# Attention on one Trainium2 core: row maxima over pairs of PSUM banks, and the matmuls of a pair issued one behind the other

## The reference, cut to what matters

```
def _attention(q, k, v, bias):
    scores = einsum('bhqd,bhkd->bhqk', q, k) / sqrt(hd)
    if bias is not None:
        scores = scores + bias[None, None]
    return einsum('bhqk,bhkd->bhqd', softmax(scores), v)

pos = arange(L)
decay_bias = -abs(pos[None, :] - pos[:, None]) * (1.0 - decay_factor)
out_short = _attention(q, k_s, v_s, decay_bias)
out_long = _attention(q, k_l, v_l, None)
out = alpha * out_short + (1.0 - alpha) * out_long      # alpha = sigmoid(mix_weight)
```

## Time and profile before

| | |
|---|---|
| median of 3 runs | 4903.04 us |
| span of the profiled execution | 4900.3 us |
| PE busy | 4717.9 us, 96% |
| DVE busy | 4038.9 us, 82% |
| ACT busy | 2978.9 us, 61% |
| attention stage, first to last V | 546.4 to 3786.9 us of the span |

### The profile page before, as it was taken

One profiled execution on the slowest core, in us unless ns is written; L12 is line 12 of the kernel. 1 busy time (PEld: TensorE's weight loads), 2 busy tenths in 40 slices (PEclk: granted clock), 3 DMA queues, 4 the chain that ended last, 5 costly groups with the idle time before them and its releaser, 6 DMA issues. The chain is left out here.

```text
span 4900.3 us, 100056 instructions
## 1 busy us (share of the span) xinstructions
PE 4717.9 (96%) x30796; PEld 2078.4 (42%) x30796; DVE 4038.9 (82%) x6609; ACT 2978.9 (61%) x5170; POOL 3278.9 (67%) x1267
## 2 busy tenths in 40 slices
PE   8998999999999999999999999999998699999998
PEld 3444333333333333333333333333332477777776
DVE  7567888888888888888888888888884488888887
ACT  3222477777777767777777777767766355555554
POOL 0000498998989989898998989989898233333332
PEclk9999799999999999999999999999999799999999
DMA  5444366666666666666666676666755100000000
GB/s 171 126 140 130 92 149 153 152 154 158 147 156 151 152 157 147 160 146 158 152 153 157 145 160 152 152 153 145 165 134 114 67 27 21 27 27 27 27 23 12
DMA packets 207465, 592.51 MB, mean 121 GB/s; under 512 B 37043, under 2 KB 110899, under 8 KB 157941
## 3 DMA queue, kind: packets, MB, share of 16 engines
q0 software_dynamic: 55008, 400.58, 37.4%
q1 hardware_dynamic: 151919, 185.58, 12.6%
q10 hardware_dynamic: 38, 0.08, 0.0%
HBM read 123.56 MB, written 61.64 MB: 38 GB/s over the span
## 5 line engine op out<-in xcount | busy, mean ns | idle before, releaser
L877 DVE TENSOR_REDUCE rowmax_parts<-scores_qk 128x1 f32<-128x512 f32 x4096 | 2525.9, 681 | 427.0 <-PE scores_qk L954 426.8
L862 ACT ACTIVATE probs_T<-scores_kq 128x512 f32<-128x512 f32 x4096 | 2288.4, 597 | 955.4 <-PE scores_kq L954 857.7
L800 POOL TENSOR_TENSOR probs_added<-probs_added,probs_T 128x2048 f32<-128x2048 f32 x510 | 2387.0, 4680 | 49.5 <-POOL probs_added L800 35.7
L954 PE MATMUL scores_kq<-q_operand,k_operand 103*128 103x512 f16 (+3 forms) x3712 | 1274.6, 349 | 19.5 <-ACT probs_T L862 17.4
L954 PE MATMUL scores_qk<-k_operand,q_operand 96*128 96x512 f16 (+4 forms) x3712 | 1121.6, 351 | 42.4 <-DMA v_operand<-v_dram 15.0
L1025 PE MATMUL outputs_T<-probs_T,v_operand 128*32 128x512 f32 x8192 | 1092.7, 605 | 1.3 <-ACT probs_T L862 1.3
L954 PEld LDWEIGHTS scores_kq<-q_operand,k_operand 103*128 103x128 f16 x3712 | 358.4, 97 | 934.6 <-ACT probs_T L862 688.0
L954 PEld LDWEIGHTS scores_qk<-k_operand,q_operand 96*128 96x128 f16 (+1 forms) x3712 | 354.6, 98 | 432.0 <-DVE rowmax_parts L877 186.6
L1650 PE MATMUL f_gate_up<-w_gate_up,xq_T 128*128 128x256 f16 (+1 forms) x4608 | 494.3, 266 | 7.7 <-DVE hidden L1541 6.6
L812 POOL DMA_DIRECT2D probs_poured<-probs_T x318 | 276.7, 870 | 266.1 <-DMA probs_poured<-probs_T 192.8
L1650 PEld LDWEIGHTS f_gate_up<-w_gate_up,xq_T 128*128 128x128 f16 x4608 | 421.4, 99 | 76.8 <-issue 24.3
(11 more groups left out here) (167 smaller groups left out, 4134.8 us busy)
## 6 DMA issues: line engine op xcount, KB each, us to landing
probs_poured<-probs_T POOLq DMA_DIRECT2D x382, 1024.0 KB, 7.6
qk_parts_dram<-qk_parts SPq DMA_DIRECT2D x96, 256.0 KB, 2.8
q_operand<-qk_parts_dram SPq DMA_DIRECT2D x192, 128.0 KB, 2.6
k_operand<-qk_parts_dram SPq DMA_DIRECT2D x192, 128.0 KB, 4.0
v_dram<-v_heads SPq DMA_DIRECT2D x16, 1024.0 KB, 6.5
v_operand<-v_dram SPq DMA_DIRECT2D x64, 256.0 KB, 6.1
q_operand_above<-qk_parts_dram SPq DMA_DIRECT2D x96, 128.0 KB, 2.9
x_groups<-x SPq DMA_DIRECT2D x8, 1024.0 KB, 9.3
```

The lines of the kernel that those rows point to most:

```text
L800: nc.gpsimd.tensor_tensor(total, first, probs[:, b % PBUF, :], ALU.add).then_inc(added.sem, 1)
L862: nc.scalar.activation(probs[:, kb % PBUF, qt * BANK:(qt + 1) * BANK], pb[:, k % 2, :], ACT.Exp)\
L877: nc.vector.reduce_max(rowmax[:, w % 2, c // NQ, c % NQ:c % NQ + 1], pa[:, k % 3, :], AX.X)\
L954: return nc.tensor.matmul(out, lhsT, rhs, start=start, stop=stop, skip_group_check=True)
```

## The change

The tile `turned` is gone, and its bank makes `scores_qk` four banks: two pairs. Two neighbouring M chunks are written into the two banks of a pair; only the first of them waits and only the second signals. VectorE reduces a pair with one instruction of 1024 elements. TensorE's order becomes V, E2, M0, M1, E3, E0, M2, M3, E1. The turning of the maxima moves from TensorE and ScalarE to VectorE, as a transpose of 32 x 32 blocks in SBUF on fp16 values, behind the first pair of step 10; each block of 32 queries is then placed by a DMA of its own, so four DMAs instead of one for each destination. VectorE's transpose waits for the negation and for the DMAs that last read the buffer it writes. GpSimd clears `negmax` once at the start. The diff, cut to its core:

```diff
-        negmax = sb("negmax", [P, 2, KB], F32)
-        maxT = sb("negmax_T", [KB, 2, P], F16)
+        negmax = sb("negmax", [P, 2, SQUARE], F16)
+        maxT = sb("negmax_T", [P, 2, SQUARE], F16)
-        pa = ps("scores_qk", [P, 3, BANK], F32)
+        pa = ps("scores_qk", [P, 4, BANK], F32)
-        pt = ps("turned", [P, BANK], F32)
...
             def place_max(w, n):
-                sp.wait_ge(roundm.sem, roundm.at(n, w + 1))
+                sp.wait_ge(turned.sem, turned.at(n, w + 1))
                 for dst in (q_op[w], q_up[w]) if w % 2 == 0 else (q_op[w],):
-                    sp.dma_start(dst[MROW:MROW + 1, :], maxT[:, w % 2, :]).then_inc(maxrow[w].sem, 16)
+                    row = dst[MROW:MROW + 1, :].rearrange("o (t b c) -> o t b c", t=KB, c=SQUARE)
+                    for b in range(P // SQUARE):
+                        sp.dma_start(row[:, :, b, :], maxT[b * SQUARE:b * SQUARE + KB, w % 2, :]).then_inc(maxrow[w].sem, 16)
...
-            def max_chunk(w, n, c):
-                nc.vector.reduce_max(rowmax[:, w % 2, c // NQ, c % NQ:c % NQ + 1], pa[:, k % 3, :], AX.X)\
+            def max_pair(w, n, g):
+                k = w * PAIRS + g
+                dve.wait_ge(scoredA.sem, scoredA.at(n, k + 1))
+                half = pa[:, 2 * (k % 2):2 * (k % 2) + 2, :].rearrange("p b q -> p (b q)")
+                nc.vector.reduce_max(rowmax[:, w % 2, g // 2, g % 2:g % 2 + 1], half, AX.X).then_inc(maxed.sem, 1)
...
+            def turn_max(w, n):
+                dve.wait_ge(maxed.sem, maxed.at(n, (w + 1) * (PAIRS + 1)))
...
+                nc.vector.transpose(maxT[:, w % 2, :], negmax[:, w % 2, :]).then_inc(turned.sem, 1)
...
             def scores_for_max(w, n, c):
-                if k >= 3:
-                    pe.wait_ge(maxed.sem, maxed.at(n, k - 2 + (k - 3) // CHUNKS))
+                if c % 2 == 0 and k >= 2:
+                    pe.wait_ge(maxed.sem, maxed.at(n, k - 1 + (k - 2) // PAIRS))
...
-                last.then_inc(scoredA.sem, 1)
+                if c % 2:
+                    last.then_inc(scoredA.sem, 1)
...
                         scores(i + 1, 2)
                         maxima(0)
+                        maxima(1)
                         scores(i + 1, 3)
-                        maxima(1)
-                        if ahead and i == TURN_MAX:
-                            turn_max(*ahead)
+                        scores(i + 2, 0)
                         maxima(2)
-                        scores(i + 2, 0)
                         maxima(3)
                         scores(i + 2, 1)
```

More of the change, by code:

```diff
@@ L583 @@
 CHUNKS = KB * NQ
+PAIRS = CHUNKS // 2
 UNITS = 4
@@ L594 @@
 TURN_MAX = 10
+SQUARE = 32
 INVERT = 7
@@ L641, in attend @@
         poured_sum = sb("probs_poured", [P, 2, L], F32)
-        rowmax = sb("rowmax_parts", [P, 2, KB, NQ], F32)
-        negmax = sb("negmax", [P, 2, KB], F32)
-        maxT = sb("negmax_T", [KB, 2, P], F16)
+        rowmax = sb("rowmax_parts", [P, 2, KB, 2], F32)
+        negmax = sb("negmax", [P, 2, SQUARE], F16)
+        maxT = sb("negmax_T", [P, 2, SQUARE], F16)
         oT = sb("o_T", [P, 2, BANK], F32)
@@ L655, in attend @@
         pc = ps("sums", [P, BANK], F32)
-        pt = ps("turned", [P, BANK], F32)
         consts = sem("a_consts")
         chain = sem("a_const_chain")
+        cleared = sem("a_negmax_cleared")
         rows = [sem(f"a_rows{i}") for i in range(2)]
@@ L664, in attend @@
         opened = [Rises(sem(f"a_opened{w}"), 10 - 3 * (w % 2), 16) for w in range(UNITS)]
-        maxrow = [Rises(sem(f"a_maxrow{w}"), 2 - w % 2, 16) for w in range(UNITS)]
-        scoredA = Rises(sem("a_scored_qk"), UNITS * CHUNKS)
-        maxed = Rises(sem("a_maxed"), UNITS * (CHUNKS + 1), credit=1)
+        maxrow = [Rises(sem(f"a_maxrow{w}"), 4 * (2 - w % 2), 16) for w in range(UNITS)]
+        scoredA = Rises(sem("a_scored_qk"), UNITS * PAIRS)
+        maxed = Rises(sem("a_maxed"), UNITS * (PAIRS + 1), credit=1)
         turned = Rises(sem("a_max_turned"), UNITS)
-        roundm = Rises(sem("a_max_rounded"), UNITS)
         scoredB = Rises(sem("a_scored_kq"), UNITS * CHUNKS)
@@ L777, in _ @@
             nc.gpsimd.memset(ones[:, :], 1.0).then_inc(consts, 1)
+            nc.gpsimd.memset(negmax[:, :, :], 0.0).then_inc(cleared, 1)
             nc.gpsimd.memset(ident[:, :], 0.0).then_inc(chain, 1)
@@ L831, in _ @@
         def _(act):
[L832 to L840, removed]
             load_positions(act, 0)
-            round_max(0, 0)
             def one_pass(n, first, last):
@@ L847, in one_pass @@
                     for kb in range(KB):
-                        if kb == (TURN_MAX + 2) % KB and after(w, n, last):
-                            round_max(*after(w, n, last))
                         u, b = divmod(w * KB + kb - PBUF, KB)
@@ L872, in _, with negate @@
         def _(dve):
-            def max_chunk(w, n, c):
-                k = w * CHUNKS + c
+            def max_pair(w, n, g):
+                k = w * PAIRS + g
                 dve.wait_ge(scoredA.sem, scoredA.at(n, k + 1))
-                nc.vector.reduce_max(rowmax[:, w % 2, c // NQ, c % NQ:c % NQ + 1], pa[:, k % 3, :], AX.X)\
-                    .then_inc(maxed.sem, 1)
[L880 to L886, removed]
+                half = pa[:, 2 * (k % 2):2 * (k % 2) + 2, :].rearrange("p b q -> p (b q)")
+                nc.vector.reduce_max(rowmax[:, w % 2, g // 2, g % 2:g % 2 + 1], half, AX.X).then_inc(maxed.sem, 1)
+            def negate(w, n):
+                dve.wait_ge(maxed.sem, maxed.at(n, (w + 1) * (PAIRS + 1) - 1))
+                nc.vector.tensor_reduce(negmax[:, w % 2, 0:KB], rowmax[:, w % 2, :, :], AX.X, ALU.max, negate=True)\
+                    .then_inc(maxed.sem, 1)
+            def turn_max(w, n):
+                dve.wait_ge(maxed.sem, maxed.at(n, (w + 1) * (PAIRS + 1)))
+                if w >= 2:
+                    dve.wait_ge(maxrow[w - 2].sem, maxrow[w - 2].at(n, maxrow[w - 2].per_pass))
+                elif not isinstance(n, int) or n > 0:
+                    s = maxrow[w + 2]
+                    dve.wait_ge(s.sem, s.before(n, s.per_pass))
+                nc.vector.transpose(maxT[:, w % 2, :], negmax[:, w % 2, :]).then_inc(turned.sem, 1)
+            for g in range(PAIRS):
+                max_pair(0, 0, g)
+            dve.wait_ge(cleared, 1)
             negate(0, 0)
-            for c in range(EARLY):
-                max_chunk(1, 0, c)
+            turn_max(0, 0)
+            for g in range(EARLY // 2):
+                max_pair(1, 0, g)
             def take(w, n):
@@ L930, in one_pass @@
                         unit = after(w, n, last, distance)
-                        for c in chunks if unit else ():
-                            max_chunk(*unit, c)
-                            if c == CHUNKS - 1:
+                        for c in chunks[::2] if unit else ():
+                            max_pair(*unit, c // 2)
+                            if c // 2 == PAIRS - 1:
                                 negate(*unit)
+                            if i == TURN_MAX and c == chunks[0]:
+                                turn_max(*ahead)
+                        if i == TURN_MAX and ahead and not unit:
+                            turn_max(*ahead)
                         if back and i == MIX and back[0] % 2:
@@ L968, in scores_for_max @@
                 t, kc = divmod(c, NQ)
-                k = w * CHUNKS + c
+                k = w * PAIRS + c // 2
                 if c == 0:
                     pe.wait_ge(opened[w].sem, opened[w].at(n, opened[w].per_pass))
-                if k >= 3:
-                    pe.wait_ge(maxed.sem, maxed.at(n, k - 2 + (k - 3) // CHUNKS))
[L975 to L978, removed]
+                if c % 2 == 0 and k >= 2:
+                    pe.wait_ge(maxed.sem, maxed.at(n, k - 1 + (k - 2) // PAIRS))
+                elif c % 2 == 0:
+                    m = UNITS * PAIRS - 2 + k
+                    pe.wait_ge(maxed.sem, maxed.before(n, m + 1 + m // PAIRS))
+                bank = pa[:, 2 * (k % 2) + c % 2, :]
                 if w % 2:
@@ L1077, in _ @@
                 scores_for_max(0, 0, c)
-            turn_max(0, 0)
             pe.wait_ge(rows[1], 16 * (7 + 2))
```

## The result

The changed kernel takes 4987.93 us (median, 4987.08 to 4997.8); its ratio to the kernel before is 1.0171, interval 1.0159 to 1.0184: 1.7% slower, 84 us against the runs of the kernel before that stood beside it (median 4903.71). The forecast was 4983.

What follows compares the result with a forecast made beforehand. The prediction took a plain step to hang on one VectorE maximum, with ScalarE's two-bank turn-round nearly as late. New steps summed to a stage of 3320 against 3240, span 4980, plus 2.7: 4983 us, range 4953 to 5045.

Steps and rivals of the forecast that it cites:

- The turn-round: ScalarE through two banks of `scores_kq`: 1.07 us from E2 to E0's load, only 0.88 of work between; E0 waits some 0.19.
- Forecast steps of 3.04, 3.16, 3.11 and 3.23: Step times in us: plain (2.93 before), with a kinked E, with a kinked M, with both kinked.
- 1.11 to 1.17 in a queue: VectorE's time in us for a queued pair of maxima: 1.11 taken, 1.17 the upper bound.
- Costing it at nothing: VectorE's work adds no time, hidden by TensorE's stalls; at the upper bound, steps 7 to 11 pile up, 13 us in all.
- the lower bound (0.22): VectorE's transpose of 32 fp16 elements in step 10: bounds 0.22 and 0.96 us, 0.22 taken, inside slack of 1.3.
- The margin of 3.3 us: Placed row there at 10.9 us with eight issues of 0.58; E0 of step 14 of an odd unit wants it at 14.2.
- no wait for `negmax_T` at E0 of step 14: Sign that the forecast is right: the placed rows arrive before E0 of step 14 needs them.
- within 2 us: Prologue: eight open DMAs, about 3.5 us more, against 32 pairs at 0.06 to 0.12 less; within 2 us of nothing.
- The sum: Units of 52.46 (even) and 51.30 (odd), 32 each, 3320.3; 3310 after deductions, plus 10: stage 3320 against 3240, 80 more.
- the 10 us allowed for disturbed steps: Allowance in the stage for three steps disturbed by a late exponential, as at 3606.60, where PE idled 3.38.
- The faster one, 4793: Turn-round shrinks below 0.88, E0 finds its bank free, plain steps 2.85, stage 3120; chance 0.08 in full, 0.04 halfway (4903).
- the fallen clock: Rival: short stalls lower TensorE's clock, 2.6 us a step in one step of twenty, 134 us, 5117; chance 0.02.

Runs made afterwards that it cites:

- easing the loop: Kernel before, with GpSimd's pour (DMA adding exponentials to a sum) of block 12 moved ahead of block 13's addition: 4896.97 us, ratio 0.9978.
- the pairs in the old order: Changed kernel with paired maxima, VectorE transpose and placing DMAs kept, TensorE's order back to E2, M0, E3, M1, M2, E0, M3, E1: 4903.68 us, ratio 0.9989.

## Why the prediction was right, and where it was not

- **The turn-round.** The step on which all hung, E0 at 1.07 behind E2 with 0.88 in front of it, was right: 1.07 and 0.42 stand unchanged in the trace after, and a third bank removes the wait with the order left as it is. (Of the old order the prediction says four chunks and lists five; its 5 x 0.22 is the right count.) Forecast steps of 3.04, 3.16, 3.11 and 3.23 measure 3.05, 3.17, 3.12 and 3.23.
- **VectorE.** A pair was put at 1.11 to 1.17 in a queue; the two of the step above take 2.35 together, and 2.35 - 1.22 = 1.13 from start to start. Step 8 above is as long as a step with a kinked M anywhere, and waits of M for VectorE are no longer in the list. Costing it at nothing was right.
- **The transpose** takes 195 ns, at the lower bound (0.22) that was chosen:

```profile
L735 SPq DMA_DIRECT2D q_operand<-negmax_T x256: 502/583/1341, 530.5 to 3814.0; - x128
L735 SPq DMA_DIRECT2D q_operand_above<-negmax_T x128: 502/1341/2400, 533.1 to 3768.6; - x128
L882 DVE STREAM_TRANSPOSE negmax_T<-negmax x64: 176/195/213, 530.3 to 3812.0; 128x32 f16<-128x32 f16 x64
...
  PE scores_kq L959: 7.2, 8
```

- **The placing.** The last lines are issue times and who waited. I took 0.58 for an issue; that is the median for `q_operand`, but for `q_operand_above` the median is 1.34 and the longest 2.40, beyond the bound of 1.38 from the earlier trace rows. The margin of 3.3 us bore most of it: PE waited 7.2 us in all, eight times, of which 4.52 in the prologue. So the sign "no wait for `negmax_T` at E0 of step 14" didn't hold in every unit: some 3 us that the sum has at nothing.
- **The prologue was mis-sized.** I put it within 2 us; V starts 4.4 later than in the earlier trace rows, which is most of the 5 us between 4983 and 4988. I had set the DMAs against a gain of the pairs, but the maxima of the first unit are no sooner turned (the transpose at 530.3, the first placing DMA at 530.54, where it was 530.0), and then E0 waits for eight DMAs in a row:

```profile
530.54 2.54 SPq L735 DMA_DIRECT2D q_operand<-negmax_T  x4
...
533.13 2.48 SPq L735 DMA_DIRECT2D q_operand_above<-negmax_T  x4
536.76 0.29 PE L959 MATMUL scores_kq<-q_operand,k_operand 103*128 103x128 f16 x1 [4.52 <-DMA q_operand_above<-negmax_T]
```

- **The sum.** 3320 were forecast for the stage and 3321.6 measured, closer than its terms, which is luck. The medians of the steps add up to 52.56 and 51.39 a unit, where 52.46 and 51.30 were forecast: 6 us in all. Of the 10 us allowed for disturbed steps about 5 came, 3 of them in step 14 of odd units, where E0 waits for the placed rows. The stalls for which the 10 were allowed did not come back: ScalarE waited for pours 30.9 us before and not at all after, since a slower TensorE lets GpSimd's pours finish in time.
- **The rivals.** The faster one, 4793, overlooked what the experiments found: even without E0's wait the stage can't go much below the pours' loop as GpSimd's program has it, near 50.5 us a unit, and the kernel before was already there (3240.5 / 64 = 50.6), with steps of its own that add up to little less, since easing the loop gave it only 10 us. The pairs in the old order end at the same 4903. Of the fallen clock nothing was seen in the changed kernel: the granted clock is a mean of 0.983 over the span (0.984 before), and 1.00 from 700 to 3500 us in both.
- By the Trainium skill, "VectorE: DVE Perf Modes", section "The TRN2 errata — SBUF-src ops pay a fixed extra latency per instruction", 1024 elements from PSUM are 120 + 1024 cycles, an estimate of 1.19 us; the row has 1.216, so the page is near for one instruction alone. Two queued maxima took 1.17 before and a queued pair takes 1.13, a saving of 0.04 where the prediction's estimate from the page was 0.125. Neither could show in the time, because VectorE was not on the path.

## What to carry to other kernels

A buffer of two banks has a turn-round: from the start of the matmul that fills a bank, through the engine that empties it, to the matmul that fills it again (here 1.07 us, the same in every step looked at, before and after). Count how much other work TensorE's written order leaves between the two, for each bank, before moving a line; four chunks instead of five cost 1.7%. And when a stall is lifted and the time stays, look for a loop of another engine with the same period: here the pairs in the old order gained 0.1% until the place of one DMA in GpSimd's order was changed, and 0.4% then.

## What the runs showed of the hardware that was not expected

SyncE's small DMAs issued one behind the other took 0.50 to 2.40 us each to issue, against 0.50 to 1.38 when there were two of them. Their number alone doesn't set it: for `q_operand_above` the median is 1.34 in the changed kernel and 0.59 in the pairs with the old order, with the same DMAs. A pour of 1 MB within SBUF lands 7.6 us after its issue in the median, and 9.3 to 9.7 us after in the two timelines above where it is waited for (issued at 1610.58, ScalarE released at 1619.97; GpSimd idle 10.15 behind the one of 1609.20). A stall of about 0.2 us in each 3 us step left TensorE's granted clock as it was (means of 0.984 and 0.983); single stalls of 2 us and more in the pairs with the old order were followed by stretches at 0.50, as at 1417.80 above.
